# Edge sum of a graph layer: the weight's parts carried in two fields a list, and VectorE's dependent operations interleaved

## The reference

```python
xn = layernorm(x)
gathered = edge_weight[:, None] * xn[src]
gnn = segment_sum(gathered, dst, num_segments=6250) + node_vec1
x = x + gnn + linear_attention(xn)
x = x + experts(layernorm(x))   # 8 experts, the best 2 of each row
```

## Time and profile before

| | |
|---|---|
| median of three runs | 2259.97 us |
| the profiled execution's own time | 2257.62 us |
| its span, first to last instruction | 2255.8 us |
| busy: PE, PE weight loads, DVE, ACT, POOL | 2091.7, 1854.7, 1950.6, 1079.5, 1455.2 us |
| mean granted TensorE clock | 0.971 of full speed |

### The profile page before, as it was taken

One profiled execution on the slowest core, in us unless ns is written; L12 is line 12 of the kernel. 1 busy time (PEld: TensorE's weight loads), 2 busy tenths in 40 slices (PEclk: granted clock), 3 DMA queues, 4 the chain that ended last, 5 costly groups with the idle time before them and its releaser, 6 DMA issues. The chain is left out here.

```text
span 2255.8 us, 45631 instructions
## 1 busy us (share of the span) xinstructions
PE 2091.7 (93%) x16549; PEld 1854.7 (82%) x16550; DVE 1950.6 (86%) x3350; ACT 1079.5 (48%) x1745; POOL 1455.2 (65%) x1356
## 2 busy tenths in 40 slices
PE   7996789999999999999999999999999639999992
PEld 4665678888888888888888888888899529999992
DVE  7998999999999999999999999999888685555551
ACT  2225644444444444444444444443222267888781
POOL 3770067777777776777777777777666135888873
PEclk9998999999999999999999999999999779999996
DMA  4642433333333333333333333333554553555556
GB/s 138 160 120 80 129 115 95 91 92 106 93 93 101 93 94 92 102 94 94 93 103 92 94 91 103 92 97 92 145 152 142 171 123 61 83 81 82 82 79 141
DMA packets 160932, 235.91 MB, mean 105 GB/s; under 512 B 54834, under 2 KB 121805, under 8 KB 160490
## 3 DMA queue, kind: packets, MB, share of 16 engines
q0 software_dynamic: 70896, 164.43, 29.2%
q1 hardware_dynamic: 75536, 55.29, 9.0%
q10 hardware_dynamic: 14314, 13.68, 1.8%
HBM read 186.46 MB, written 53.24 MB: 106 GB/s over the span
## 5 line engine op out<-in xcount | busy, mean ns | idle before, releaser
L837 POOL DMA_INDIRECT picked<-xn_dram,place x1029 | 1048.1, 1019 | 538.4 <-issue 283.6
L935 PE MATMUL bank<-picked,pick_w 128*128 128x256 f32 x2058 | 500.1, 379 | 0.0
L1047 ACT COPY stage<-bank 128x512 f32<-128x512 f32 x343 | 200.9, 586 | 599.6 <-PE bank L923 593.8
L935 PEld LDWEIGHTS bank<-picked,pick_w 128*128 128x128 f32 x2058 | 391.0, 190 | 53.2
L931 PE MATMUL bank<-window,stage 128*128 128x256 f32 x1568 | 381.4, 386 | 0.0
L1307 DVE TENSOR_TENSOR hot_w<-hots,bank 128x1536 bf16<-128x1536 bf16 x343 | 327.2, 954 | 11.8
L1001 ACT COPY field_rep<-fields 128x1666 bf16<-128x1666 bf16 (+1 forms) x193 | 322.3, 1675 | 1.2 <-DVE vals L1184 1.2
L931 PEld LDWEIGHTS bank<-window,stage 128*128 128x128 f32 x1568 | 282.6, 190 | 30.3
L1303 DVE TENSOR_TENSOR hots<-ends,bank 128x1408 bf16<-128x1408 bf16 x343 | 301.5, 879 | 0.0
L923 PE MATMUL bank<-hot_w,hots 128*128 128x128 bf16 x4116 | 285.6, 219 | 2.4 <-DVE hot_w L1307 2.0
L931 PE MATMUL bank<-stage 128*128 128x256 f32 x1176 | 286.0, 386 | 0.0
(11 more groups left out here) (253 smaller groups left out, 3262.5 us busy)
## 6 DMA issues: line engine op xcount, KB each, us to landing
picked<-xn_dram,place POOLq DMA_INDIRECT x1029
w<-in_L_ffn_W_dram SPq DMA_DIRECT2D x16, 512.0 KB, 8.7
xn_dram<-xn ACTq DMA_DIRECT2D x49, 128.0 KB, 2.0
xT_dram<-xT ACTq DMA_DIRECT2D x49, 128.0 KB, 2.1
base_dram<-acc SPq DMA_DIRECT2D x7, 896.0 KB
sum_dram<-acc SPq DMA_DIRECT2D x7, 896.0 KB
z_dram<-vals SPq DMA_DIRECT2D x7, 896.0 KB
out_dram<-sum_dram SPq DMA_DIRECT2D x1, 6250.0 KB, 22.5
```

Source lines behind the costliest of these rows:

```text
L837: pool.indirect_dma_start(out=picked[:, i % SETS * PICK + q, :], out_offset=None, in_=xn_dram, in_offset=bass.IndirectOffsetOnAxis(ap=plac ...
L935: mm = pe.matmul(sum_ps[pp], pick_w[i % SETS][:, q, :], picked[:, i % SETS * PICK + q, :], start=False, stop=(q == PICK - 1))
L1047: act.copy(block_sb[pp].rearrange("p j c -> p (j c)"), banks[pp][:, :]).then_inc(a_copied, 1)
```

## The change

**Three fields instead of four.** The float32 weight's upper 16 bits go into field W as they are, its lower 16 bits into a new field LOW, offset by 4096 with bit 14 taken out; that bit travels in the top bit of END. `vals` and the table have 147 columns instead of 196, and there is one multiplication by `hot_t` and one repeated field fewer.

**Front.** `apart` gets two more operations a chunk (`low_k`, `bit_e`) at its step 0; `weight_part` has three operations a chunk instead of five (a strided copy, an addition, an addition that puts the bit into `src_r`), and VectorE's END field now waits for the last of them instead of for its own cuts.

**Decoding.** ScalarE copies two rows of the table and the raw table for a dense list (two copies, was one), and three copies for a picked list (was two); `raw` is now used by both kinds, with a wait (`raw_free`). VectorE joins the halves of the weight: a dense list costs eight operations (was two), a picked list six (was five), in three or four pieces between other work.

**Order on VectorE.** The loop over tiles is now hots for tile i+2, picks for tile i+1, hot_w (now `weigh`) for tile i+2, add for tile i-1. The three rank operations stand at i = 2 as: rank_add between picks and weigh, rank_fold between weigh and add, rank_sum last. In the ramp the decoding of the last list (`part` or `make_list`) stands between the last `values` and `hot_tiles`, and the rest of it around `add_mix` and `slots`.

The diff, cut to its core (PARTS stays 3; the waits on `listed` are counted anew):

```diff
@@ -41,8 +41,8 @@
-FIELDS = 4
-END, W = 0, 1
+FIELDS = 3
+END, W, LOW = 0, 1, 2
...
@@ -315,15 +315,17 @@
-                at, part = slice(c * UN, (c + 1) * UN), n // 2
+                at = slice(c * UN, (c + 1) * UN)
...
-                else:
-                    pool.wait_ge(parts, 5 * c + n)
-                if n % 2 == 0:
-                    pool.tensor_copy(fields[:, W + part, at, :], weight[:, at, :]).then_inc(parts, 1)
-                else:
-                    pool.tensor_tensor(weight[:, at, :], weight[:, at, :], fields[:, W + part, at, :], ALU.subtract).then_inc(parts, 1)
+                    high = weight[:, at, :].rearrange("p g c -> p (g c)").bitcast(U16)[:, 1:2 * UN * CH:2]
+                    pool.tensor_copy(fields[:, W, at, :].bitcast(U16).rearrange("p g c -> p (g c)"), high).then_inc(parts, 1)
+                elif n == 1:
+                    pool.wait_ge(cut, 6 * c + 2)
+                    pool.tensor_scalar(fields[:, LOW, at, :].bitcast(U16), low_k[:, :, :], float(LOWEST * P), None, ALU.add).then_inc(parts, 1)
+                elif n == 2:
+                    pool.wait_ge(cut, 6 * c + 6)
+                    pool.tensor_tensor(src_r[:, :, :], src_r[:, :, :], bit_e[:, :, :], ALU.add).then_inc(parts, 1)
...
@@ -538,6 +540,10 @@
+                        dve.wait_ge(parts, 3 * c)
+                    bits = weight[:, at, :].bitcast(I32)
+                    dve.tensor_scalar(low_k[:, :, :], bits, 0xBFFF, None, ALU.bitwise_and).then_inc(cut, 1)
+                    dve.tensor_scalar(bit_e[:, :, :], bits, 0x4000, 1, ALU.bitwise_and, ALU.logical_shift_left).then_inc(cut, 1)
@@ -548,11 +554,11 @@
                 elif m == 4:
-                    dve.wait_ge(cut, 4 * c + 3)
+                    dve.wait_ge(cut, 6 * c + 5)
...
-                    dve.wait_ge(cut, 4 * c + 4)
+                    dve.wait_ge(parts, 3 * c + 3)
...
@@ -660,7 +666,8 @@
-        pair = sb("pair", [P, NB])
+        halves = sb("halves", [P, 2, NB], I32)
+        upper = sb("upper", [P, NB], I32)
...
@@ -997,7 +1004,7 @@
                 if later(s):
-                    act.wait_ge(vals_done, 3 * s - (2 if b <= 2 else 1 if b <= 3 else 0))
+                    act.wait_ge(vals_done, FIELDS * (s - 1) + b)
@@ -1018,15 +1025,27 @@
-                at = table[par][:, AT_SRC:ROWS, :, :].rearrange("p (f j) b h -> p f j b h", j=DENSE)[:, :, j, :, :]
-                act.copy(at, table_ps.unsqueeze(3).broadcast_to([P, FIELDS, NB, 2])).then_inc(unpacked, 1)
+                at = table[par][:, AT_SRC:ROWS, :, :].rearrange("p (f j) b h -> p f j b h", j=DENSE)[:, 0:2, j, :, :]
+                act.copy(at, table_ps[:, END:W + 1, :].unsqueeze(3).broadcast_to([P, 2, NB, 2]))
+                raw_free(s)
+                act.copy(raw[:, :, :], table_ps).then_inc(unpacked, 1)
+            def raw_free(s):
+                g, k = divmod(s, GRP)
+                if k % 2:
+                    act.wait_ge(parted, DENSE * g + k // 2 + 1)
+                elif k:
+                    act.wait_ge(listed, PICK * g + k // 2)
+                elif g:
+                    act.wait_ge(parted, DENSE * g)
...
-                if later(n):
-                    act.wait_ge(listed, 3 * n)
+                act.copy(weight[par][:, :, bass.ds(q, 1)].rearrange("p b a -> p (a b)"), table_ps[:, W, :])
+                raw_free(s)
@@ -1048,20 +1067,20 @@
+                repeat_fields(s, 1, 2)
...
-                repeat_fields(s, 3, FIELDS)
...
-                repeat_fields(s + 1, 0, 2)
+                repeat_fields(s + 1, 0, 1)
...
-                act.wait_ge(listed, 3 * PICK)
+                act.wait_ge(listed, PICK)
@@ -1087,14 +1106,14 @@
+                        repeat_fields(s, 1, 2)
+                    if more and i == 1:
...
-                    if more and i == 1:
-                        repeat_fields(s, 3, FIELDS)
...
-                            act.wait_ge(listed, (g + 2) * 3 * PICK)
+                            act.wait_ge(listed, (g + 2) * PICK)
@@ -1104,8 +1123,6 @@
-                    if more and i == 6:
-                        repeat_fields(s + 1, 1, 2)
...
@@ -1155,11 +1172,23 @@
+                rank_add(s)
+                rank_fold(s)
+                rank_sum(s)
+            def rank_add(s):
...
+            def rank_fold(s):
...
+            def rank_sum(s):
@@ -1189,7 +1218,40 @@
-                dve.tensor_scalar(both, both, P - 1, 0x3F80, ALU.bitwise_and, ALU.bitwise_or).then_inc(parted, 1)
+                dve.tensor_scalar(both, both, P - 1, 0x3F80, ALU.bitwise_and, ALU.bitwise_or)
+                halve(s)
+            def splits_of(s):
+                g, k = divmod(s, GRP)
+                return 3 * (g * DENSE + (k + 1) // 2) + g * PICK + k // 2
+            def halve(s):
+                dve.tensor_scalar(halves[:, 0, :], raw[:, LOW, :].bitcast(I32), 16, None, ALU.logical_shift_right)
+                dve.tensor_scalar(halves[:, 1, :], raw[:, END, :].bitcast(I32), 17, 0x4000, ALU.logical_shift_right, ALU.bitwise_and).then_inc(split, 1)
+            def join(s, low_bits):
+                dve.wait_ge(split, splits_of(s) + 1)
+                return dve.scalar_tensor_tensor(out=low_bits, in0=halves[:, 0, :], scalar=float(-LOWEST * P), in1=halves[:, 1, :], op0=ALU.add, op1=ALU.add)
+            def part_join(s):
+                join(s, raw[:, W, :].bitcast(U16)[:, 0:2 * NB:2]).then_inc(split, 1)
+            def part_cut(s):
+                dve.wait_ge(split, splits_of(s) + 2)
+                dve.tensor_scalar(upper[:, :], raw[:, W, :].bitcast(I32), 8, 8, ALU.logical_shift_right, ALU.logical_shift_left).then_inc(split, 1)
+            def part_weights(s, j, par):
+                dve.wait_ge(split, splits_of(s) + 3)
+                first, second, third = (table[par][:, AT_SRC + n * DENSE + j, :, :] for n in (1, 2, 3))
+                whole, most = (of.unsqueeze(2).broadcast_to([P, NB, 2]) for of in (raw[:, W, :], upper[:, :].bitcast(F32)))
+                dve.tensor_tensor(second, most, first, ALU.subtract)
+                dve.tensor_tensor(third, whole, most, ALU.subtract).then_inc(parted, 1)
@@ -1197,12 +1259,15 @@
-                dve.tensor_scalar(row[:, :], raw[:, END, :].bitcast(I32), 23, None, ALU.logical_shift_right).then_inc(listed, 1)
-                dve.tensor_tensor(pair[:, :], raw[:, W, :], raw[:, W + 1, :], ALU.add).then_inc(listed, 1)
-                dve.wait_ge(listed, 3 * n + 2)
+                dve.tensor_scalar(row[:, :], raw[:, END, :].bitcast(I32), 23, 0xFF, ALU.logical_shift_right, ALU.bitwise_and)
+                halve(s)
+            def place_list(s, n, q, par):
+                low_bits = weight[par][:, :, :].rearrange("p b q -> p (b q)").bitcast(U16)[:, 2 * q:2 * NB * PICK:2 * PICK]
+                join(s, low_bits)
...
-                                  first_row[:, bass.ds(s, 1)].broadcast_to([P, NB]), ALU.add)
-                dve.tensor_tensor(weight[par][:, :, bass.ds(q, 1)].rearrange("p b a -> p (a b)"), pair[:, :], raw[:, W + 2, :], ALU.add).then_inc(listed, 1)
+                                  first_row[:, bass.ds(s, 1)].broadcast_to([P, NB]), ALU.add).then_inc(listed, 1)
@@ -1276,23 +1341,31 @@
-                values(s, 0, 2)
+                values(s, 0, 1)
...
-                values(s, 2, 3)
+                values(s, 1, 2)
...
-                values(s, 3, FIELDS)
-                hot_tiles(s + 1)
-                if later(s):
-                    add_mix(t + 2)
-                slots(s)
+                values(s, 2, 3)
...
+                hot_tiles(s + 1)
+                if s % 2 == 1:
+                    part_join(s - 1)
+                elif s > 0:
+                    place_list(s - 1, s // 2 - 1, s // 2 - 1, 0)
+                if later(s):
+                    add_mix(t + 2)
+                if s % 2 == 1:
+                    part_cut(s - 1)
+                slots(s)
+                if s % 2 == 1:
+                    part_weights(s - 1, (s - 1) // 2, 0)
@@ -1303,6 +1376,11 @@
+            def weigh(t, i):
+                of = cur_of(i)
+                to = hot[i % SETS]
@@ -1320,8 +1398,10 @@
+                hots(1, 1, None)
+                weigh(0, 0)
...
-                hots(1, 1, None)
+                weigh(1, 1)
@@ -1339,10 +1419,6 @@
                 for i in range(BU):
-                    if i + 1 < BU:
-                        picks(t + i + 1, i + 1)
-                    elif after:
-                        picks(t + BU, 0)
@@ -1351,6 +1427,20 @@
+                    if i + 1 < BU:
+                        picks(t + i + 1, i + 1)
+                    elif after:
+                        picks(t + BU, 0)
+                    if more and i == 2:
+                        rank_add(s)
+                        if odd == par:
+                            part_cut(s - 1)
+                    if i + 2 < BU:
+                        weigh(t + i + 2, i + 2)
+                    elif after:
+                        weigh(t + i + 2, i + 2 - BU)
```

(21 more changed lines are left out.)

9 lines of the change are left out of this document (4 added, 5 removed).

## The result

The changed kernel takes 2325.16 us (median of four runs, 2317.8 to 2331.56) where the kernel before takes 2257.81 us in the same measurement (2254.19 to 2261.45): a ratio of 1.030, 95% interval 1.028 to 1.032. The forecast was 2228.9 us. It is slower by 67 us where 31 us less were expected.

What follows compares the result with a forecast made beforehand. TensorE was taken to bound the units, VectorE the ramp and front. The terms -28.1 - 5.7 + 2.7 = -31.1 us, on the median 2259.97 us, gave 2228.9 us; own range 2222.7 to 2238.9, 8-in-10 range 2221 to 2241.

Steps and rivals of the forecast that it cites:

- Part 1: TensorE's table in 42 units: 147 columns take 2.23 us instead of 2.90, a gain of 28.1 us.
- rival of the weight loads: TensorE's narrow table is bound by its weight loads, units gain nothing: 2257 us, 4 per cent.
- Part 2: VectorE in the units: its own unit falls from 29.88 to 28.3 us, worth nothing on the path by itself.
- rival that ended slower: VectorE becomes the bound at i = 1 to 3 of the units through the decoding: 2272 us, 3 per cent.
- Part 3: Moved steps on VectorE and ScalarE's extra copy in the units delay nothing: 0 us.
- Part 4: The ramp of 8 steps, where VectorE's time is the time: a gain of 5.7 us.
- Part 5: The front: two more operations in each of seven chunks at 0.19 us, a loss of 2.7 us.

Runs made afterwards that it cites:

- experiment 8: Changed kernel with three fields and new decoding, but VectorE's order of before (picks, hots, weigh; rank operations together): 2223.38 us, ratio 0.986.
- experiment 11: Changed kernel with the ramp of slot numbers copied once into PSUM, so slots reads one input from SBUF and one from PSUM: 2223.08 us, ratio 0.985.
- experiment 1: Changed kernel with weigh straight behind hots again in the tile loop (hots, weigh, rank_add and cut, picks): 2221.7 us, ratio 0.984.
- experiment 9: Changed kernel with the three rank operations together at the end of i = 2, weigh still behind picks: 2222.53 us, ratio 0.985.
- experiment 3: Changed kernel with one memset of 48 columns on VectorE between weigh and the add in each tile: 2222.09 us, ratio 0.985.
- experiment 10: Changed kernel with one memset of 49 columns on VectorE behind acc's addition, just ahead of the sorting operation, in each tile: 2223.24 us, ratio 0.985.
- experiment 4: Changed kernel with one gather a tile instead of three, every matmul kept on the first row's data: 2222.13 us, ratio 0.985.
- experiment 2: Kernel before, four fields and old decoding, with only the tile loop's order changed to hots, picks, hot_w: 2255.41 us, ratio 0.9992.

## Why the prediction was wrong

**Part 1** (28.1 us from TensorE's units) held: 2.26 us for the table against 2.23, and the unit without GpSimd in the way falls from 30.03 to 29.39 us, 0.64 against 0.67. The rival of the weight loads is out: 34 different loads with 147 columns go at 2.26 / 34 = 66.5 ns a pair. The Trainium skill (TensorE: Matmul & The Clock Gate, Back-to-back issue gap) has 81 ns for 128 columns; the trace doesn't agree, here for different loads too.

**Part 2** held for VectorE, 28.3 us of its own as forecast. Its last sentences failed. "That cover is what is late next: TensorE, then VectorE 1.1 us behind it, then GpSimd: its gathers take 883.9 + 238.5 us of 41 units, 27.4 us each ... of which 2.0 are left." This took 27.4 us as a property of the gathers. It is not: 1028 ns was the mean of the earlier trace rows, the gathers that nothing disturbs take 945, and the difference, 0.08 us in 21 gathers or 1.7 us a unit, was stalling beside VectorE, set by where VectorE's operations fall. The change moved all of them. The failed step is this: the dealing out that I priced as -0.84 and -0.23 us of VectorE's time, "worth nothing on the path by itself", took GpSimd from 27.8 to 32.0 us, where the same three fields in the old order leave it at 28.3 us (experiment 8). TensorE's 29.4 us covered 1.6 of these 4.2 us; the other 2.6 stood on the path. The times say the same: 2325 - 2222 = 103 us, 2.5 us for each of 41 units.

The rival that ended slower put the bound on VectorE at 3 per cent. None named GpSimd. Two things could have led there. In the earlier trace rows the mean isn't the duration of any gather: a view in order of time would have shown most at 0.95 us (704 of 860 under 0.97) and one in seven at 1.3 to 2.0. And the Trainium skill (SBUF — State Buffer, Who interferes with whom) states that a VectorE instruction with two SBUF inputs contends with a GpSimd instruction that reads SBUF. The traces agree, with 3.31 us beside `slots` in the changed kernel and 0.94 us in experiment 11. The same page of the Trainium skill (SBUF: two separate sides) has it that whichever starts first gets the shared ports for the whole instruction. The traces agree in that a gather held up by one operation of 1.03 us takes 1.85 us; but in the changed kernel gathers that begin up to 0.02 us ahead of `slots` by the records wait for two operations of VectorE. The section Who interferes with whom of the Trainium skill's page also has it that `tensor_tensor` did not stall DMAs in an earlier probe, and infers that making descriptors needs only the write interface; the gathers here are stalled by it, and these runs decide.

**Part 3** put the moved steps at nothing. What it checked held: TensorE waited 0.7 us for `hot_w` over the units by its weight loads. The zero itself failed, by the step above: "No DMA is added or moved" is true of the program, but the moved steps of VectorE lengthened the gathers, and putting them back in another order (experiments 1, 8 and 9) gives 102 to 103 us. **Part 4**, the ramp: from the start of the edge sum to the first base 129.0 us before (177.95 to 306.93), 123.5 after (181.25 to 304.76), 5.5 us less for 5.7 forecast. **Part 5**, the front: 181.25 - 177.95 = 3.3 us more for 2.7. The two added operations stand 0.19 to 0.20 us apart as priced:

```profile
67.08 0.28 DVE L545 TENSOR_SCALAR low_kept<-weight 128x238 int32<-128x238 int32 x1 [0.99 <-DMA weight<-in_edge_weight_dram]
67.28 0.28 DVE L546 TENSOR_SCALAR bit_to_end<-weight 128x238 int32<-128x238 int32 x1
67.47 0.28 DVE L553 TENSOR_SCALAR dst_t<-dst_i 128x238 int32<-128x238 int32 x1
```

But one profile can't hold Part 5 to a microsecond: with the same front, the first base of the runs above begins anywhere from 299.2 to 304.8 us. Over all runs ramp and front together gained some 5 us, not 3. (The terms of the forecast's range add up to 2223.1 us at its lower end, not 2222.7.) Where the forecast's 31.1 us became 35.3 (2257.0 less 2221.7 us), in the span of experiment 1: 26.4 us in the units by ScalarE's casts (27.4 forecast for 41), 5.0 us ahead of them (3.0), 1.9 us behind the last base (0.7), in all 33.3; the rest is the scatter of single executions. The other 2.9 us between 2228.9 and 2221.7 are that of the median it was put on, 2259.97 us.

## What to carry to other kernels

Before an engine's unit is taken as fixed, look at the single durations: a mean above the common value is time spent behind someone else, and it moves when that engine's order moves. Here a VectorE operation with both inputs in SBUF holds a gather for as long as it runs; one input in PSUM (experiment 11) ends that. A change of order by 0.01 to 0.12 us (experiments 1, 3 and 10) ended the loss here as well, but which way it turns out could not be told beforehand. The best of these kernels keeps the change's three fields and puts weigh straight behind hots: 2221.7 us, 1.6 per cent under the kernel before; its time is level with that of experiments 3, 4 and 8 to 11, so TensorE is its bound.

## What the runs showed that was not expected

- An indirect gather beside a two-input SBUF operation of VectorE takes 1.8 to 1.9 us for 0.95 (operation of 1.03 us), and 3.31 us beside a back-to-back pair of 2.48 us. One that begins 0.1 us into the pair gets in between its halves (2.01 us).
- In the changed kernel each stall puts the gather after next 2.45 us behind VectorE's `hots`, and the tile's own work takes 2.46 us, and the gather at `slots` takes 3.3 us in 41 of 42 units. Experiments 2, 9 and 11 have the same 2.46 us without the chain.
- A gather that begins with a sorting operation can pass or lose at the same recorded start. Where it passes, VectorE pays: a half of `slots` takes 1.31 to 1.35 us in experiment 1 for 1.28.
- One more operation of 0.1 us a tile on VectorE, or 0.12 us more waiting a tile, makes the changed kernel 102 to 103 us faster.
- Loads of 34 different weights with 147 moving columns go at 66.5 ns a pair at a granted clock of 0.98 to 1.00.
